# The second attention layer's loop: row maximum ahead of the low halves, output products four turns behind the scores, fillers in the first turns, the low-rank sum in the last four

## The reference, cut to what matters

```
h = _layernorm(x)                                # 1024 rows of 512
hidden = concatenate([context, h], axis=1)
q = h @ Wq.T; k = hidden @ Wk.T; v = hidden @ Wv.T   # 16 query heads, 4 key heads, 96 wide
scores = einsum('bkgqd,bksd->bkgqs', q, k) * scale
attn = softmax(scores)
out = einsum('bkgqs,bksd->bkgqd', attn, v)
x = x + out @ Wo.T
x = x + (_layernorm(x) @ (W + low-rank sum).T + bias)
```

## Time and profile before

| | |
|---|---|
| runs, median | 873.93 us |
| profiled execution, time | 875.48 us |
| its span, first to last instruction | 873.7 us |
| TensorE busy | 846.7 us (97%) |
| VectorE, ScalarE, GpSimd busy | 56%, 40%, 35% |
| granted TensorE clock, mean | 0.996 |
| chain that ended last, TensorE's share | 82% |

### The profile page before, as it was taken

One profiled execution on the slowest core, in us unless ns is written; L12 is line 12 of the kernel. 1 busy time (PEld: TensorE's weight loads), 2 busy tenths in 40 slices (PEclk: granted clock), 3 DMA queues, 4 the chain that ended last, 5 costly groups with the idle time before them and its releaser, 6 DMA issues.

```text
span 873.7 us, 12372 instructions
## 1 busy us (share of the span) xinstructions
PE 846.7 (97%) x4758; PEld 701.8 (80%) x4758; DVE 487.3 (56%) x876; ACT 351.7 (40%) x827; POOL 303.3 (35%) x232
## 2 busy tenths in 40 slices
PE   6999999999999999999999999999989999999998
PEld 5788787787887887887877778888978888888776
DVE  5866654654754754654665736465144544555674
ACT  5342221321221322222213142565677666766542
POOL 3386534634534634524525330110121111211132
PEclk9899999999999999999999999999999999999999
DMA  8123211311211311211211122000020100210002
GB/s 286 46 73 86 61 49 27 107 50 33 82 45 37 107 39 40 83 37 48 74 37 46 50 77 79 25 25 13 13 73 25 38 25 26 98 48 1 1 1 97
DMA packets 24891, 48.15 MB, mean 55 GB/s; under 512 B 3584, under 2 KB 4736, under 8 KB 24704
## 3 DMA queue, kind: packets, MB, share of 16 engines
q1 hardware_dynamic: 24400, 47.22, 18.0%
q10 hardware_dynamic: 432, 0.14, 0.1%
HBM read 45.12 MB, written 2.23 MB: 54 GB/s over the span
## 4 chain that ended last, share of the span: by engine, by line
PE 82%; ACT 9%; DVE 4%; DMA 2%; issue 1%; POOL 1%; SPq 0%; POOLq 0%; ACTq 0%; DVEq 0%
PE PB L1101 21%; PE PB L1103 21%; PE PB L1102 21%; PE PB L1259 5%; PE PB L1164 3%; PE PB L1190 2%; ACT Eb L849 2%; PE PB L1108 2%; PE PB L1274 2%; PE PB L1291 2%; DMA stage<-in_wo 2%; DVE Ol L1072 1%; ACT Oh L720 1%; PE PB L1174 1%; DVE sm L1054 1%
## 5 line engine op out<-in xcount | busy, mean ns | idle before, releaser
L881 DVE TENSOR_TENSOR xs<-xs,PB 128x512 f32<-128x512 f32 x112 | 76.7, 686 | 91.9 <-PE PB L1103 85.8
L679 POOL TENSOR_TENSOR qb<-qb,arena 128x512 f32<-128x512 f32 x64 | 82.8, 1294 | 128.9 <-DVE arena L959 128.5
L1101 PE MATMUL PB<-WOh,Oh 128*128 128x512 f32 x256 | 99.9, 390 | 0.0
L1102 PE MATMUL PB<-WOl,Oh 128*128 128x512 f32 x256 | 99.9, 390 | 0.0
L1103 PE MATMUL PB<-WOh,Ol 128*128 128x512 f32 x256 | 99.8, 390 | 0.0
L720 ACT ACTIVATE Oh<-PB 128x512 fp32r<-128x512 f32 (+2 forms) x160 | 69.3, 468 | 57.7 <-PE PB L1190 39.7
L1101 PE MATMUL PB<-xTh,WQh 128*128 128x512 f32 x192 | 77.9, 405 | 1.8 <-DVE xTl L933 1.8
L1103 PE MATMUL PB<-xTh,WQl 128*128 128x512 f32 x192 | 75.8, 395 | 0.0
L1102 PE MATMUL PB<-xTl,WQh 128*128 128x512 f32 x192 | 75.7, 394 | 0.0
L990 DVE TENSOR_TENSOR Ol<-PB,Oh 128x512 fp32r<-128x512 f32 x64 | 39.8, 684 | 63.5 <-ACT Oh L720 63.4
L670 POOL TENSOR_TENSOR WQl<-stage,WQh 128x512 fp32r<-128x512 f32 x38 | 49.0, 1291 | 75.1 <-ACT WQh L720 74.4
(11 more groups left out here) (203 smaller groups left out, 2054.1 us busy)
## 6 DMA issues: line engine op xcount, KB each, us to landing
stage<-in_wq SPq DMA_DIRECT2D x44, 256.0 KB, 2.9
stage<-in_wo SPq DMA_DIRECT2D x44, 256.0 KB, 2.6
arena<-recs SPq DMA_DIRECT2D x32, 256.0 KB, 3.9
stage<-in_wk SPq DMA_DIRECT2D x14, 256.0 KB, 2.7
arena<-in_ctxT SPq DMA_DIRECT2D x8, 256.0 KB, 5.7
stage<-in_wv SPq DMA_DIRECT2D x8, 256.0 KB, 3.1
xs<-in_x SPq DMA_DIRECT2D x8, 256.0 KB, 6.3
out<-xs SPq DMA_DIRECT2D x8, 256.0 KB, 2.0
```

The source lines that it names most:

```text
L679: e.tensor_tensor(dst, dst, tmp, ALU.add).then_inc(s_radd)
L881: e.tensor_tensor(xs[:, i, :], xs[:, i, :], PB[b][:, :], ALU.add).then_inc(free[b])
L1101: e.matmul(dst, Ah, Bh, start=(k == 0), stop=False)
L1102: e.matmul(dst, Ah, Bl, start=False, stop=False)
```

## The change

The loop runs from turn 1. A turn is now c1(it-2), b1(it-1), fillers, e1(it-4), d1(it-2). The old step `d1` keeps TensorE's and ScalarE's part; VectorE's low halves are a step of their own, `low1(it-3)`, and stand between the maximum and the new step `norm1(it-1)` (reciprocal and product). v1(1,3) to v1(1,7) and k1(0,1,1) go into turns 1 to 4, weight splits to the ends of turns, weff(0) to weff(3) with their splits into turns 29 to 32, the statistics of tiles 0 to 3 into turns 28 to 31, and their `rstd` to the loop's end. The first three output-weight blocks are split before the loop, one of them into a free buffer. Ahead of the loop, two transposes go in front of k1(2,0,0), and mgT(1) in front of v1(0,7). After the loop, both first xn stand in front of e1(29), low1(31) between two transposes, and dense(0) in front of the statistics of the last four tiles. Nothing is computed that was not computed before, and nothing is left out.

```diff
@@ -231,8 +231,6 @@
...
         step("q1", g, part)
-        if part and g % 2 == 1 and g // 2 + 1 < 4:
-            split("wq1", g // 2 + 1, part - 1)
 
...
@@ -259,9 +257,9 @@
...
         mid(i)
-    k1(2, 0, 0)
     for i in (2, 3):
         ffn_xT(i)
+    k1(2, 0, 0)
     step("rstd", 1, 4)
...
@@ -300,77 +298,88 @@
...
         step("xsplit", 2, i)
+        if i == 1:
+            stage("mgT", 1)
         if i < 2:
             v1(0, 6 + i)
-        if i == 1:
-            split("wk1", 0, 1)
-        if i == 2:
-            stage("mgT", 1)
     for i in HI:
...
     step("rstd", 2, 4)
+    split("wk1", 0, 1)
     for part in range(4):
         q1(0, part)
+        if part:
+            split("wo1", 0, part - 1)
     normed(2, HI, [lambda i=i: v1(1, i) for i in range(3)], [lambda: k1(0, 1, 0)])
-    v1(1, 3)
-    k1(0, 1, 1)
-    split("wk1", 1, 1)
-    v1(1, 4)
 
...
         ring.remove(b)
-    k1_plan = {4: (1, 1, 0), 8: (1, 1, 1), 12: (2, 1, 0), 16: (2, 1, 1)}
-    for it in range(N1 + 1):
+    v1_plan = {1: (3, 4), 2: (5,), 3: (6, 7)}
+    k1_plan = {4: (0, 1, 1), 8: (1, 1, 0), 11: (1, 1, 1), 15: (2, 1, 0), 19: (2, 1, 1)}
+    wk1_plan = {4: (1, 1), 11: (2, 1)}
+    wo1_plan = {8: (1, 0), 9: (1, 1), 10: (1, 2), 12: (2, 0), 13: (2, 1), 19: (2, 2), 20: (3, 0), 21: (3, 1), 27: (3, 2)}
+    for it in range(1, N1 + 1):
         if 0 <= it - 2:
             stage("c1", it - 2, bank=3)
-        if 0 <= it - 1 < N1:
-            stage("b1", it - 1, bank=2)
-        if it < 3:
-            v1(1, 5 + it)
-        if it in (3, 8, 16, 24):
-            split("wo1", it // 8, 0)
-            split("wo1", it // 8, 1)
-        if 1 <= it <= 28:
-            q1((it + 3) // 4, (it - 1) % 4)
+        stage("b1", it - 1, bank=2)
+        if 0 <= it - 3:
+            step("low1", it - 3)
+        step("norm1", it - 1)
+        for i in v1_plan.get(it, ()):
+            v1(1, i)
         if it in k1_plan:
             k1(*k1_plan[it])
-            if it == 8:
-                split("wk1", 2, 1)
-        if 0 <= it - 5:
-            stage("e1", it - 5)
-        if it == N1 - 4:
-            split("wo1", 3, 2)
-        elif it % 8 == 4:
-            split("wo1", it // 8, 2)
+        if it <= 28:
+            q1((it + 3) // 4, (it - 1) % 4)
+        if 0 <= it - 4:
+            stage("e1", it - 4)
         if 0 <= it - 2:
             stage("d1", it - 2, bank=4 + it % 2)
+        if it in wk1_plan:
+            split("wk1", *wk1_plan[it])
+        g, part = (it + 3) // 4, (it - 1) % 4
+        if part and g % 2 and g < 7:
+            split("wq1", g // 2 + 1, part - 1)
+        if it in wo1_plan:
+            split("wo1", *wo1_plan[it])
         if it == N1 - 6:
             step("weff_load")
-        if it in (28, 30, 32):
-            stage("weff", (it - 28) // 2)
-            step("weff_split", (it - 28) // 2)
-        if N1 - 2 <= it:
-            step("stats", 3, it - (N1 - 2))
+        if N1 - 4 < it:
+            stage("weff", it - 29)
+            step("weff_split", it - 29)
+        if N1 - 4 <= it < N1:
+            step("stats", 3, it - 28)
+    step("bias")
+    step("rstd", 3, 0)
+
 
     ring[0:0] = [2]
-    stage("e1", 28)
     stage("c1", N1 - 1, bank=3)
-    step("stats", 3, 3)
-    step("rstd", 3, 0)
+    for i in range(2):
+        step("xn", 3, i)
+    stage("e1", 29)
     stage("d1", N1 - 1, bank=5)
+    step("low1", N1 - 2)
     ring[0:0] = [3]
     ring += [4, 5]
-    stage("weff", 3)
-    step("bias")
-    stage("e1", 29)
-    normed(3, LO, [lambda: step("weff_split", 3), lambda: stage("e1", 30), lambda: stage("e1", 31)])
+    for i in LO:
+        stage("xT", 3, i)
+        if i < 2:
+            step("xn", 3, i + 2)
+        step("xsplit", 3, i)
+        if i == 0:
+            step("low1", N1 - 1)
+        if i == 1:
+            stage("e1", 30)
+    for i in LO:
+        step("add_bias", i)
+    stage("e1", 31)
+    stage("dense", 0)
     for i in HI:
...
     step("rstd", 3, 4)
-    for i in LO:
-        step("add_bias", i)
-    for i in range(3):
+    for i in (1, 2):
         stage("dense", i)
...
@@ -491,8 +500,9 @@
...
                     (more[0][:, 0:384], more[1][:, 0:384]), (WOh[:, 0, 0:384], WOl[:, 0, 0:384])]
-        wo1_home = [(WOh[:, c, :], WOl[:, c, :]) for c in range(3)] + [
-            (WVh[:, c:c + 512], WVl[:, c:c + 512]) for c in (0, 512)]
+        wo1_home = [(WOh[:, c, :], WOl[:, c, :]) for c in (1, 2, 0)] + [
+            (WVh[:, c:c + 512], WVl[:, c:c + 512]) for c in (0, 512)] + [(more[2], more[3])]
+        wo1_at = (0, 1, 5, 2, 3, 4, 0, 1, 2, 3, 4, 0)
         we_home = [(WQh[:, m, :], WQl[:, m, :]) for m in range(3)] + [(WKh[:, :], WKl[:, :])]
...
@@ -575,7 +585,7 @@
...
             r0 = 384 * k[0] + 128 * k[1]
-            return a["wo1"][r0:r0 + 128, :], 512, *wo1_home[(3 * k[0] + k[1]) % 5]
+            return a["wo1"][r0:r0 + 128, :], 512, *wo1_home[wo1_at[3 * k[0] + k[1]]]
 
...
@@ -597,8 +607,9 @@
...
                 return ("q1", 2 * j - 1, m) if j else (("k1", 1, 0, 1), ("k1", 2, 0, 1), ("q0", 15, 2))[m]
-            n = 3 * k[0] + k[1] - 5
-            return ("e1", 8 * (n // 3) + 7) if n >= 0 else ("v1", 1, 7)
+            n = 3 * k[0] + k[1]
+            return (("e0", 15, 3), ("v1", 1, 7), ("e1", 7), ("e1", 15), ("e1", 23))[
+                0 if n < 3 else 1 if n < 6 else 2 if n < 8 else 3 if n < 11 else 4]
 
...
@@ -1046,18 +1057,22 @@
...
                     e2 = s % 2
-                    mx, rs, rr = sm[:, e2, 0, 0:4], sm[:, e2, 0, 4:8], sm[:, e2, 1, 0:4]
-                    E3 = Eb[:, e2, :].rearrange("p (b t) -> p b t", b=4)
+                    mx = sm[:, e2, 0, 0:4]
                     dve.wait_ge(*done("b1", s))
...
                                     negate=True).then_inc(s_max)
+                elif kind == "norm1":
+                    s, = k
+                    e2 = s % 2
+                    rs, rr = sm[:, e2, 0, 4:8], sm[:, e2, 1, 0:4]
+                    E3 = Eb[:, e2, :].rearrange("p (b t) -> p b t", b=4)
                     dve.wait_ge(*read("b1", s))
...
                     e.tensor_tensor(E3, E3, rr.unsqueeze(2).broadcast_to([128, 4, 128]), ALU.mult).then_inc(s_nrm1)
-                elif kind == "d1":
+                elif kind == "low1":
                     s, = k
...
@@ -1303,7 +1318,7 @@
...
                         pe.wait_ge(*lo_ready("wo1", j, m))
-                        last = thrice(PB[b][:, :], m, 3, Ohp[:, os, col], Olp[:, os, col], *wo1_home[(3 * j + m) % 5])
+                        last = thrice(PB[b][:, :], m, 3, Ohp[:, os, col], Olp[:, os, col], *wo1_home[wo1_at[3 * j + m]])
                     last.then_inc(full[b])
...
```

## The result

The changed kernel takes 888.6 us in the median of four runs (885.4 to 890.5), the kernel before 875.0 in four (the three behind the 873.93 of the forecast and one more); the ratio is 1.016, 95% interval 1.014 to 1.018. It is slower by 13.6 us. Forecast were 879.5 us, 5.6 us more than before, in a range that ended at 884.5. The sign was right; the forecast change was less than half of the measured one.

A forecast was written before the change was run, and what follows sets the result against it. TensorE was taken to bound the kernel, so only its waits could change the time. Gone 10.5 us, new 13.6 and 2.5 for the clock: net +5.6 on 873.9, so 879.5 us, range 874 to 884.5.

The forecast's parts named there:

- What bounds the kernel: Whole kernel: TensorE, busy 846.7 of 873.7 us; with the same matmuls, time can move only by TensorE's waits.
- Gain: Loop's first part and middle: an earlier maximum and fillers in turns 1 to 4 remove five waits, 4.7 us.
- rival 4: Turns 3 to 6: probabilities still late, so the early gains of 4.7 us don't come; 884.2 us, chance 0.10.
- rival 3: Even turns and behind the loop: low halves early enough, e1 does not wait; 871.1 us, chance 0.08.
- ahead of the loop: Before the loop: shorter waits at mid(2) and at the second delta, 1.2 us gained at each.
- ScalarE's part at nothing: Loop turns: weight splits at a turn's end push the exponential by less than the 1.2 us gained; costed at nothing.
- The new wait in even turns: Eleven even turns: e1 waits 0.17 us each for low halves made in the same turn; +1.9 us, bounds 0 and 3.9.
- Turns 30 and 32: Loop's end: without q1, e1 right behind b1 waits for the same turn's low halves; 2.35 us each, +4.7 us.
- Behind the loop: After the loop: new waits at tile 0's transposes +1.0 us, at e1(30) +4.0 us, at tile 4 +2.0 us.
- The clock: At e1(30): TensorE's granted clock falls behind the long gap; +2.5 us, bounds 0 and 5.
- Rival 1: At e1(30): same waits, but the clock holds; +3.1 us, 877.0 us, chance 0.22.
- Rival 2: Turns 30 and 32: the clock falls there as well, up to 2.5 us each; 884.5 us, chance 0.10.

The follow-up runs named there:

- low_at_end: Changed kernel with VectorE making the low halves of it-2 right behind d1(it-2) in all turns, as before the change: 880.3 us, ratio 1.007.
- k1_turns: Changed kernel with the k1 tiles of turns 11, 15 and 19 and one weight split moved one turn later: 886.1 us, ratio 1.013.
- low_first: Changed kernel with the low halves ahead of the maximum again in turns 29 to 32 alone: 888.7 us, ratio 1.015.
- tail_low: Changed kernel with d1(31)'s high halves ahead of both first xn and low1(31) ahead of tile 0's xTl, behind the loop: 883.9 us, ratio 1.010.
- stats_first: Changed kernel with the statistics of tiles 4 to 7 and rstd ahead of dense(0) again: 885.6 us, ratio 1.012.
- spin: Changed kernel with 37 needless matmuls in front of e1(26), e1(28) and e1(30): 885.6 us, ratio 1.012.
- five_behind: Changed kernel with e1 five turns behind the scores instead of four, and statistics of tiles 0 to 3 one turn later: 884.3 us, ratio 1.010.
- five_shift: Changed kernel with e1 five turns behind and the four weight splits that follow an e1 one turn later too: 877.7 us, ratio 1.0031.

## Why the prediction was wrong in size

Three terms failed: the wait of e1 in even turns was sized at 1.9 us and cost 4.8; the bank that e1 is handed in turns 11, 15 and 19 stood nowhere in the sum and cost 2.7; the clock behind turn 30 was put at nothing and cost 1.6. The other paths were read rightly or nearly so.

**What bounds the kernel.** Right. Everything the change did shows as waits of TensorE and as its clock.

**Gain.** Right in amount: no wait of c1, d1 or b1 is left, and rival 4 is refuted (rival 3 too, by the waits of e1). Half wrong in its reason: the prediction named the maximum's earlier start and the fillers of turns 1 to 4; low_at_end shows that turns 1 to 28 do not need the first. The 2.6 us ahead of the loop are read from the waits that are gone; no run takes that part of the change back.

**ScalarE's part at nothing, and the turns with k1.** The prediction costed ScalarE's splits "at nothing" and took k1 as cover only. I considered ScalarE making the exponential late, and not the bank that e1 is handed. A turn with k1 uses three tiles of the ring of four, and in turns 11, 15 and 19 the fourth tile back is the q1 tile that ends in this very turn and is evacuated last. It cost 2.7 us, and k1_turns took it away by a shift of one turn. Before the change all k1 of the loop stood in turns 4, 8, 12 and 16, in which no q1 tile begins; moving them to 11, 15 and 19 was enough. The order of the instructions shows such a bank, their durations don't.

**The new wait in even turns.** The mechanism was right, each of the eleven turns pays; the term was mis-sized, 0.17 us where 0.44 was paid. The maximum started 1.09 us after b1 as forecast (721.12 for 720.03), but the low halves followed 0.73 us later and not 0.61, and TensorE started 0.15 us after their end and not 0.05:

```profile
721.12 0.69 DVE L1064 TENSOR_REDUCE sm<-PB 128x4 f32<-128x512 f32 x1 [1.44 <-PE PB L1289]
721.85 1.29 DVE L1087 TENSOR_TENSOR Ol<-PB,Oh 64x256 fp32r<-64x256 f32 x3
```

```profile
723.29 0.47 PE L1116 MATMUL PB<-WOh,Oh 128*128 128x512 f32 x1
```

The prediction let VectorE start the low halves 0.09 us before the maximum's end; here they start 0.04 after it. Each slip is a tenth, and eleven turns multiply them. The bounds, 0 to 3.9, missed it too. The estimate of 0.20 us per turn from the Trainium skill (TensorE: Matmul & The Clock Gate, section on LDWEIGHTS) missed it for the same reason: the exposed weight load is only the smaller part. e1's first matmul takes 0.30 to 0.31 us to the next where 0.23 is usual, 0.08 us for it.

**Turns 30 and 32.** 4.7 forecast, 5.1 paid. The queue in front of the low halves is the one the prediction counted, and low_first shows that taking the maximum out of it shortens each wait by only half a microsecond.

**Behind the loop.** e1(30) 4.0 and 4.2, tile 4 2.0 and 2.0: right, by the queue orders named, and each shown by an edit that removes it (tail_low, stats_first). Tile 0: 1.0 and 1.6. Its xn starts 12.2 us after b1 of turn 32 and not 10.95, and most of that is rstd, forecast at the 2.38 us of before: it took 3.35 (839.75 to 843.10). One of its twelve small operations, 0.16 us long elsewhere, lasted until GpSimd had finished the low half of the last weight:

```profile
840.58 1.29 POOL L718 TENSOR_TENSOR WKl<-w1T,WKh 128x512 fp32r<-128x512 f32 x1 [7.25 <-ACT WKh L731]
```

```profile
840.75 1.14 DVE L931 TENSOR_TENSOR lnb<-lnb 128x4 f32<-128x4 f32 x1
```

The change had put that split beside rstd; before, GpSimd stood idle during it. No run moves the split away, so its share of the wait is read from the timeline and not shown by an edit.

**The clock.** The fall at e1(30) was forecast at 2.5 us and cost 1.7 in this execution, 2.3 in k1_turns (17.58 us from e1(30) to tile 4, where spin, with its clock held, takes 15.26); spin shows it to be a price of idling. Rival 1, that it holds, is refuted. Rival 2 was half right, and its half is one that varies: behind the wait of 2.34 us in turn 30 the clock fell in all four profiles that had this wait (changed kernel, k1_turns, tail_low, stats_first), and in low_first behind 1.76 us; behind the 2.27 us in turn 32 in two of the four (k1_turns, stats_first); and behind the 1.84 us ahead of tile 4, which rival 2 left out, in four of nine (k1_turns, five_behind, five_shift, low_at_end). I had charged it a chance of one in ten as a thing that happens or doesn't; it was a cost to be put in by expected value at every gap of about 2 us, some 3 us in all.

**The sum.** 7.4 us were missing in the trace: 2.9 from the even turns, 2.7 from the bank, 1.6 from the clock of turn 30, 1.2 from e1(26), e1(28), tile 0 and e1(30), less 0.8 for the clock at e1(30) and 0.2 ahead of the loop. The range left no room for a cost that nobody had looked for.

What stays open is why the clock falls behind one gap and not behind an equal one. The Trainium skill (TensorE: Matmul & The Clock Gate, Part 1) says that the chip judges activity on a schedule of its own, not aligned with the kernel. The spread between the runs does not speak against it; no run here moves that schedule, so it is not shown.

## What to carry to other kernels

When a consumer is moved one turn nearer to its producer, walk the queue of every engine between them in the turn where nothing stands in front of the consumer; and move with it all that is timed by it, weight splits into its operands and the banks it is handed among them. If the late operand feeds only some of a call's products, do the others first: that took back 11 of 13.6 us without moving a step. And count each new idle stretch of TensorE of some 2 us as longer than it is: here the clock fell behind more than half of them. A fall cost about 1.6 us, the one at the 4 us gap up to 2.5.
